# Scores and values of a cross-attention in four bands of TensorE, row normalisation on ScalarE, value blocks in one VectorE operation, and a new order of the background jobs in a mixture-of-experts stage

## The reference

```python
x = x + tanh(g_xattn[0]) * L0_xattn(layernorm(x), ctx)   # this change
x = x + tanh(g_ffn[0])   * L0_ffn(layernorm(x))          # 8 experts, top 2 of them
x = x + tanh(g_xattn[1]) * L1_xattn(layernorm(x), ctx)
x = x + tanh(g_ffn[1])   * L1_ffn(layernorm(x))          # quantised weights and rows

def L0_xattn(query, key_value, ...):     # 16 heads of 16 channels, 77 keys
    q = (query @ Wq + bq); k = (key_value @ Wk + bk); v = (key_value @ Wv + bv)   # split into heads
    attn = softmax(clip(einsum('bhqd,bhkd->bhqk', q, k) * scale, -CLAMP, CLAMP))
    return einsum('bhqk,bhkd->bqhd', attn, v) @ Wo + bo
```

## Time and profile before

| | us |
|---|---|
| median of 3 runs | 1237.63 (1236.72 to 1238.66) |
| the profiled execution, its own time | 1235.38 |
| its span | 1233.5 |
| TensorE busy | 1122.2 (91%) |
| VectorE busy | 917.2 (74%) |
| ScalarE busy | 834.9 (68%) |
| GpSimd busy | 526.1 (43%) |

### The profile page before, as it was taken

How to read it: one execution, slowest core, us unless ns; L and a number is a source line. 1 busy time by engine, 2 the same in 40 slices (tenths; PEclk the granted TensorE clock), 3 DMA queues, 4 the chain that set the end, 5 groups by cost and what they waited for, 6 DMA issues and landing times. The chain is left out here.

```text
span 1233.5 us, 25073 instructions
## 1 busy us (share of the span) xinstructions
PE 1122.2 (91%) x8279; PEld 847.2 (69%) x8279; DVE 917.2 (74%) x2065; ACT 834.9 (68%) x2413; POOL 526.1 (43%) x499
## 2 busy tenths in 40 slices
PE   6899999996894999999999999839999999869798
PEld 4788888884553677777777776617777777635476
DVE  4978888874755566666666668848999999769798
ACT  3677777772573556556665566539888888559897
POOL 3767777762125221222221211048888888500000
PEclk9999999997997999999999999979999999979899
DMA  5333333216964144333333333252433333000134
GB/s 137 88 95 104 103 103 99 89 62 185 289 175 157 56 69 161 114 108 119 117 116 121 115 98 114 79 159 84 125 103 118 100 122 95 25 2 1 35 112 129
DMA packets 127420, 132.04 MB, mean 107 GB/s; under 512 B 23209, under 2 KB 111583, under 8 KB 127167
## 3 DMA queue, kind: packets, MB, share of 16 engines
q1 hardware_dynamic: 119901, 112.17, 30.0%
q0 software_dynamic: 6480, 17.70, 5.2%
q10 hardware_dynamic: 914, 0.59, 0.2%
HBM read 82.78 MB, written 47.64 MB: 106 GB/s over the span
## 5 line engine op out<-in xcount | busy, mean ns | idle before, releaser
L1504 ACT ACTIVATE exp_h<-exp_ps_h,exp_b_now 128x256 f32<-128x256 f32 (+1 forms) x320 | 124.4, 439 | 148.4 <-PE exp_ps_h L1441 144.4
L1405 POOL DMA_INDIRECT exp_xg<-xn,all_token_of x71 | 84.5, 1190 | 309.9 <-PE exp_ps_x L1420 294.8
L1441 PE MATMUL exp_ps_h<-exp_xhi,exp_w_now 128*128 128x256 bf16 (+1 forms) x1280 | 198.3, 265 | 10.6 <-DVE exp_xlo L1534 10.6
L1886 ACT ACTIVATE a_z<-a_ps_sc,a_nmx 128x77 f32<-128x77 f32 x512 | 159.1, 367 | 33.5 <-DVE a_nmx L1988 33.5
L1441 PE MATMUL exp_ps_h<-exp_xlo,exp_w_now 128*128 128x256 bf16 (+1 forms) x640 | 163.2, 265 | 0.0
L1609 DVE TENSOR_TENSOR exp_hlo<-exp_h,exp_hhi 128x512 bf16<-128x512 f32 (+1 forms) x160 | 99.2, 632 | 77.7 <-ACT exp_hhi L1508 75.8
L1441 PEld LDWEIGHTS exp_ps_h<-exp_xhi,exp_w_now 128*128 128x128 bf16 x1280 | 121.7, 100 | 25.6 <-issue 13.0
L1454 PE MATMUL exp_ps_y<-moe_w2s,exp_hhi 128*128 x568 | 134.2, 379 | 1.7 <-DVE exp_y L1626 1.7
L1886 ACT ACTIVATION_READ_ACCUMULATOR a_z<-a_ps_sc,a_nmx 128x1 f32 x512 | 127.4, 249 | 0.0
L1853 PE MATMUL a_ps_o<-a_v_now,a_phi 128*128 128x256 bf16 (+1 forms) x640 | 106.6, 273 | 2.3 <-DVE a_plo L1977 2.3
L1837 PE MATMUL a_ps_sc<-a_k_now,a_xhi 128*128 128x462 bf16 (+1 forms) x384 | 98.4, 341 | 2.1 <-DVE a_xlo L1935 2.1
(11 more groups left out here) (266 smaller groups left out, 2738.4 us busy)
## 6 DMA issues: line engine op xcount, KB each, us to landing
a_stage<-in_L_ffn_W_dram SPq DMA_DIRECT2D x64, 256.0 KB, 3.3
y_slots<-exp_y SPq DMA_DIRECT2D x71, 128.0 KB, 1.7
fold_k<-route_kst SPq DMA_DIRECT2D x16, 308.0 KB, 4.3
fold_v<-route_vst SPq DMA_DIRECT2D x16, 308.0 KB
exp_job_in<-fold_k SPq DMA_DIRECT2D x14, 352.0 KB, 3.3
exp_job_in<-fold_v SPq DMA_DIRECT2D x14, 352.0 KB, 3.2
a_x<-in_x_dram SPq DMA_DIRECT2D x32, 128.0 KB, 2.7
x<-a_xo SPq DMA_DIRECT2D x32, 128.0 KB, 1.7
```

Source lines behind the costliest of these rows:

```text
L1405: pool.indirect_dma_start(out=xg[:, v, u, :], out_offset=None, in_=xn_dram[:, :], in_offset=bass.IndirectOffsetOnAxis(ap=at.bitcast(U32), ...
L1441: mm = pe.matmul(hidden[:, i, f % 2, slots(j)], w1_now[:, v, k, hl, f * P:(f + 1) * P], xx[:, k, slots(j)], start=(q == 0), stop=(q == len ...
L1504: ins = act.activation(h[:, f, slots(j)], hidden[:, i, f % 2, slots(j)], ACT.Gelu_apprx_tanh, bias=b1_now[:, v, f:f + 1])
L1886: ins = act.activation(z[:, u, h * KEYS:(h + 1) * KEYS], ps_sc[:, j, (h - SB[j][0]) * KEYS:(h - SB[j][0] + 1) * KEYS], ACT.Exp, bias=nmx[: ...
```

## The change

1. Scores in four row bands. `kblk` keeps, for each band of 32 partitions (2 heads), only the 154 columns of these 2 heads; a tile's scores are 8 matmuls of 32 partitions and 154 columns, on four bands in turn, into four PSUM banks. ScalarE's and VectorE's semaphores count them once a tile; maxima and scores minus maximum are one operation each in place of three.
2. Values in four column bands. 17 matmuls whose stationary side is 32 columns wide, ordered so that neighbours go to different bands (`turns`). `vblk` is built by one operation in place of two, from a mask `vmask4` that GpSimd prepares.
3. The heads stand in another order, so `wv` is loaded by 6 transfers in place of 3 (pieces of 32 elements).
4. `ps_p` has two banks in place of three: chunks 8 and 9 of the transposed p go to bank 0 again, after the first copy, and are written after the transpose of the rows. Their copy is one operation in place of two.
5. The rows are normalised on ScalarE (`normal`, after exp) as x * rstd + shift; VectorE computes only `shift` = -mean * rstd (one column).
6. `place_values` is cut in two: stores in slots 0 and 5, loads in slots 1 and 7.
7. In `experts` the 28 split pieces come last: jobs 0 to 3 as before, 4 to 6 `w_out`, 7 to 10 `w_in`, 11 to 38 the pieces.

```diff
+    blocks = [(c, q, i) for c in range(RCH) for i, q in enumerate((first_of[c], first_of[c] + 1))
+              if q < ng * LANES and c * P < (q + 1) * PAIR and (c + 1) * P > q * PAIR]
+    turns = [i for row in itertools.zip_longest(*lanes) for i in row if i is not None]
...
-                    for j, (a, _) in enumerate(SB):
-                        wait(pe, s["z_done"], NSB * (T - 1) + j + 1)
...
+                    wait(pe, s["z_done"], T)
+                    for g in range(ng):
+                        for j in range(LANES):
+                            lane = slice(32 * j, 32 * j + 32)
+                            mm = pe.matmul(ps_sc[:, j, g * PAIR:(g + 1) * PAIR], qT[lane, g, :], kblk[lane, b % 2, g, :],
+                                           start=True, stop=True)
+                    mm.then_inc(s["scores_done"], 1)
...
+                    for j in range(2):
+                        wait(pe, s["pT_done"], 3 * (T - 3) + 3 - j)
+                        turn_p(T - 2, j)
                 if has(T + 1):
                     turn_x(T + 1)
                 if has(T - 2):
+                    pe.wait_ge(s["pT_done"], 3 * (T - 2) + 1)
+                    turn_p(T - 2, 2)
...
+                    for i in turns:
+                        c, q, half = blocks[i]
+                        j, g = q // ng, q % ng
+                        if c // 4 >= ready:
+                            pe.wait_ge(s["pT_done"], 3 * (T - 2) + c // 4 + 1)
+                            ready = c // 4 + 1
+                        mine = [cc for cc, qq, _ in blocks if qq == q]
+                        mm = pe.matmul(ps_v[32 * j:32 * j + 32, g * P:(g + 1) * P], vblk[0:n, bv % 2, c, half, :], pT[0:n, c, :],
+                                       start=(c == mine[0]), stop=(c == mine[-1]))
...
+            def normal(T, u, r):
+                act.wait_ge(s["shift_done"], T + 1)
+                wait(act, s["turned_x"], T)
+                act.activation(xn[:, :], x[:, r, :], ACT.Identity, scale=rstd[:, u:u + 1],
+                               bias=shift[:, u:u + 1]).then_inc(s["xn_done"], 1)
...
-                dve.tensor_scalar(xn[:, :], x[:, r, :], mv[:, u, 0:1], rstd[:, u:u + 1], ALU.subtract,
-                                  ALU.mult).then_inc(s["xn_done"], 1)
+                dve.tensor_scalar(shift[:, u:u + 1], mv[:, u, 0:1], rstd[:, u:u + 1], -1.0, ALU.mult,
+                                  ALU.mult).then_inc(s["shift_done"], 1)
...
-    SPLIT0 = AMAX0 + F // COLS_IN
-    OUT0 = SPLIT0 + PIECES
+    OUT0 = AMAX0 + F // COLS_IN
     IN0 = OUT0 + len(WROWS)
     WHALVES = 2 * KD
-    JOBS = IN0 + WHALVES
+    SPLIT0 = IN0 + WHALVES
+    JOBS = SPLIT0 + PIECES
```

More of the change, by code:

```diff
@@ L181, in attention @@
             "p (b c d) -> p b c d", b=B, c=RCH)
[L182 to L185, removed]
+        kmask8 = m.sb("kmask8", [P, hpg])
+        kmask = m.sb("kmask", [P, 2])
+        vmask = m.sb("vmask", [P, RCH, HEADS])
+        kblk = m.sb("kblk", [P, 2, ng, PAIR])
+        vmask4 = m.sb("vmask4", [P, RCH, 4])
+        vblk = m.sb("vblk", [P, 2, RCH, 2, 32])
         x = m.sb("x", [P, RING, D])
@@ L190, in attention @@
         rstd = m.sb("rstd", [P, 2])
+        shift = m.sb("shift", [P, 2])
         xn = m.sb("xn", [P, D])
@@ L363, in turn_x, with turn_p @@
                 mm.then_inc(s["turned_x"], 1)
+            def turn_p(T, j):
+                for c in range(4 * j, min(RCH, 4 * j + 4)):
+                    n = min(P, ROWS - c * P)
+                    mm = pe.transpose(ps_p[0:n, j % 2, c % 4 * P:(c % 4 + 1) * P], z[:, T % NZ, c * P:c * P + n], C.ident[:, :])
+                mm.then_inc(s["turned_p"], 1)
             def keys(b0, b1, bank):
@@ L398, in slot @@
                     pe.wait_ge(weights_in, 16 * N_WEIGHTS)
-                    values(0, 2)
+                    values(0, 1)
                 if has(T - 3):
@@ L408, in slot @@
                         pe.wait_ge(s["k_done"], b + 1)
-                    for j, (a, _) in enumerate(SB):
-                        wait(pe, s["z_done"], NSB * (T - 1) + j + 1)
-                        for jj, g, h0, h1 in pieces:
-                            if jj == j:
-                                mm = pe.matmul(ps_sc[:, j, (h0 - a) * KEYS:(h1 - a) * KEYS], qT[:, g, :],
-                                               kblk[:, b % 2, g, (h0 - g * hpg) * KEYS:(h1 - g * hpg) * KEYS],
-                                               start=True, stop=True)
-                        mm.then_inc(s["scores_done"], 1)
+                    wait(pe, s["z_done"], T)
[5 more added lines that the diff above has]
+                    mm.then_inc(s["scores_done"], 1)
                 if has(T - 2):
@@ L469, in v_copy @@
                 act.activation(v_rows[:, 2 * pair:2 * pair + 2, :].rearrange("p b d -> p (b d)"),
-                               ps_p[0:KEYS, 2 - pair, :], ACT.Copy).then_inc(s["v_rows_done"], 1)
+                               ps_p[0:KEYS, 1 - pair, :], ACT.Copy).then_inc(s["v_rows_done"], 1)
+            normal(0, 0, 0)
             turned(0)
@@ L494, in slot @@
                     act.activation(zt, zt, ACT.Exp, scale=-scale).then_inc(s["exp_done"], 1)
+                if has(T + 1):
+                    normal(T + 1, 1 - u, (t + 1) % RING)
                 if has(T):
@@ L1293, in outputs_before @@
         def outputs_before(n):
-            sizes = [0 if q < SPLIT0 else 2 if q < OUT0 else 1 for q in range(n) if q % 2 == n % 2]
+            sizes = [0 if q < OUT0 else 1 if q < SPLIT0 else 2 for q in range(n) if q % 2 == n % 2]
             return 16 * sum(sizes)
```

171 lines of the change are left out of this document (83 added, 88 removed).

## The result

The changed kernel takes 1218.32 us (median of 4 runs, 1217.24 to 1218.64), the kernel before 1237.18 (1236.61 to 1238.66) beside it: 18.9 us less, a ratio of 0.9845, 95% interval [0.983, 0.986]. The forecast was 1206.6 with a range of 1191 to 1224. The profiled execution took 1218.13 us, its span is 1216.3, 17.2 shorter than before.

A forecast was written before the change was run, and what follows sets the result against it. The prediction took TensorE to bound `attention`, then a loop through ScalarE and TensorE. Slots -29, end -2, start +2 and jobs -2 sum to -31 us, from a median of 1237.6 to 1206.6; range 1191 to 1224.

The forecast's parts named there:

- rival 1: `attention` loop longer than its parts: copies wait in three places, mode changes cost 0.3 us each; 1221 us, chance 0.14.
- Score bands: Score matmuls in `attention`: four overlapping row bands take 0.85 us a slot in place of 2.34.
- Value bands: Value matmuls in `attention`: 34 in four column bands need about 0.95 us in place of 2.53.
- The chain: Loop from relu to next relu over ScalarE and TensorE in `attention`: 7.14 us a slot, before 7.92.
- `normal` at 0.30: Normalising the rows on ScalarE, inside the `attention` loop: 0.30 us to the next instruction.
- The query projection: TensorE in the `attention` loop, behind the values: 1.06 us with its end, 0.03 to ScalarE, after 0.20 for mode change.
- Late transposes: Two transposes of p behind its first copy in `attention`: 0.38 us and 0.18 to start and be seen.
- rival 3: TensorE's pauses in `attention` lower its clock: 1.45 us a slot, if everywhere +42 us, 1249 us; chance 0.06.
- Start: Start of `attention`: `wv` needs six transfers in place of three, and tile 0 waits for them; +2 us.
- Pause of slot 5: Disturbed slots of `attention` vanish, as the piece is late no more: 6.4 us of the 29.0 gained in slots.
- Jobs: Job order in `experts`: single steps -4.4 us, pair steps +2.3, net -2.
- Rival 5: Moved jobs in `experts` cost 3 us each in pair steps, give nothing back; 1213 us, inside the forecast's 0.70 chance.

The follow-up runs named there:

- lane_order: The changed kernel with score and value band matmuls issued all of one band, then all of the next; 1261.5 us, ratio 1.0206.
- fill: The changed kernel with 8 more unused transposes of a constant per slot where TensorE waits for the normalised rows; 1211.0 us, ratio 0.9806.
- norm_vector: The changed kernel with the rows of a tile normalised on VectorE again, as before; 1195.4 us, ratio 0.9677.
- place_only: The kernel before with only the cut of `place_values` into stores (slots 0 and 5) and loads (slots 1 and 7); 1230.8 us, ratio 0.9960.
- jobs_only: The kernel before with only the new order of the jobs in `experts`; 1228.1 us, ratio 0.9936.

## Why the prediction was right, and what it missed

Direction, bound and place were right, and the time is inside the range, but 12 us from the forecast and nearer to rival 1 (1221).

- **Score bands:** 0.81 us for 0.85. The price holds, and by the four that start at once so does the picture of four bands side by side; that they must be issued in turn doesn't, since lane_order costs them nothing.
- **Value bands:** 1.33 us from start to next start. The prediction says 0.95 for this, but its own prices, 34 x 25 ns and 0.2 for the change of mode, make 1.05. Where all four bands have work the matmuls are 27 ns apart. The mean of 39 holds the change of mode as well, turns with fewer than four bands, and the wait for the last copy. On the chain, from the last copy to the query projection, 1.23 (191.07 - 189.84) for 1.19.
- **The chain:** it is the forecast's, instruction by instruction, 7.45 us for 7.14. The step that failed is `normal` at 0.30: 0.49 in the slot shown. It was read from a copy without scale and bias from memory, and rows 2 held a nearer one, the queries with a bias. That is 5.5 of the 9 us that the slots fell short. The query projection takes 1.20 to ScalarE for 1.09, 3.2 us. The prediction took its 1.06 from rows 2, where full matmuls stand ahead of it. Behind the bands it takes 1.16: its second instruction starts 0.21 us after the first, where all others are 0.11 apart. So this change of mode costs the 0.20 that were charged and 0.10 more. The piece, 0.52 for 0.50, hardly counts.
- **Late transposes:** I had charged them, inside 1.15 us. From first to last copy 1.10 us pass, 0.05 less than forecast. Before, the instruction behind the two copies started 0.97 us behind the first. Here it starts 0.03 us behind the end of the late transposes (189.81), so they cost about 0.13 us a slot, 3.8 in all, which the forecast held.
- **`normal` ahead of the transposed rows:** in slot 1 TensorE waits 2.07 us for it. The forecast took that slot to be 5.7 us as before; it is 7.64. By fill's 6.49 with the same wait, 0.8 of the 1.9 us that no term held are this wait, and 1.1 the low clock behind it.
- **Clock:** rival 3's mechanism came true in 2 slots of 30 at 1.5 us each, its price being 1.45, and in slot 1 at 1.1. The clock was low at the start of slot 2 as well, but that slot's 7.53 us are those of fill, with the clock at 1.00. It did not come true everywhere.
- **Start:** +2 as forecast, but not by its reason alone. With the same start, tile 1's scores came at 24.89 us in fill and at 28.17 in norm_vector, against 24.54 in place_only with the old one. In the changed kernel the projection of the values and the first scores, at 20.91, still ran at the longer spacing of the lower level (1.41 us for 0.81; the granted clock has its first record at about 25 us). TensorE waited 0.46 us for the last of the transfers in the changed kernel, and not at all in fill; the rest is when the clock rises.
- **Pause of slot 5:** gone, as forecast, worth 4.9 us alone.
- **Jobs:** pair steps +0 for +2.3. They stay at 10.88 us, since VectorE has time to spare there. Single steps -5.3 up to the last of them, for -4.4: 6.01 each, the w_in steps a little, too. Rival 5 failed. Its 1213 had kept the 4.4 us of the single steps, against its words "gives back nothing"; without them it is 1218, just what was measured, so that only jobs_only, and the pair steps of 10.88, rule it out.
- **`routing` and the first pair steps:** +3.4 for 0. The rows show the lower clock for longer there, 0.81 and 0.88 for 0.83 and 0.91 in the first third and the rest of `routing`, and in the second pair step the matmuls keep the longer spacing for 2.6 us more. From the first matmul of `routing` to that of `experts`, with the same code, 100.3 to 102.7 us pass in eleven other kernels of this study, 101.85 before, and 104.15 here. What puts it there was not tried.

So rival 1 named the size and a smaller part of the cause: the change of mode on the chain did cost 0.3 us a slot, 3 us in all more than charged, but no copy waited three times, and most of the chain's excess is `normal`. 9.0 us are in the chain, 4.1 in the low clock (3.0 in the long slots, 1.1 in slot 1), 0.8 in slot 1's wait: the 14 us by which the slots missed.

## What to carry to other kernels

When a faster engine hands the bound to a loop over several engines, each instruction inside that loop costs all the time to the next start, whatever the busy shares say, so work that is moved to "the idle engine" must go to the place in its list where it waits, not merely to its list. The same `normal` cost 14 us inside the loop and nothing three places earlier in ScalarE's list. Price such an instruction from a row with the same operands.

## What the runs showed of the hardware

- Scale and bias from memory add 0.09 to 0.10 us each to a ScalarE operation of 128x256 (0.30, 0.40, 0.49).
- f32 matmuls with 32 stationary columns, 34 instructions: 1.33 us in turns over four column bands (27 ns apart where all four have work), 2.61 us grouped by band (110 ns within a band, at most two bands at once); full ones are 115 ns apart. With 32 rows and 154 columns the order of the bands made no difference (0.81 and 0.83 us for 16).
- From the last column-band matmul to the first full one 0.20 us pass, and 0.10 more before the second (a projection of 1.16 us for 1.06).
- A VectorE TENSOR_SCALAR of 128x16 takes 0.11 us, or until GpSimd's running operation ends (0.60, 0.95).
- Of 28 like slots of 7.45 us two lost the clock, 14 slots apart; at 6.45, 6.96, 7.27 and 7.36, and at 7.45 with unused transposes in TensorE's wait, none of the steady ones did. With values grouped by band, at 8.73, eight in a row did.
